# An expert layer on one core: a loop over experts, and an unrolled program with two chunks of the second product in plain fp32

## The reference, what is computed

```python
h = gelu(x @ Wi[e] + bi[e])          # 64x256 @ 256x1024
o = h @ Wo[e] + bo[e]                # 64x1024 @ 1024x256
r = o + x
y = (r - mean(r)) * rsqrt(var(r) + 1e-12) * gamma[e] + beta[e]
```

## Time and profile before

| What | Value |
|---|---|
| Median of three runs | 149.77 us |
| Span of the profiled execution, first to last instruction | 147.0 us |
| Busy PE / DVE / ACT / POOL | 118.9 / 115.8 / 76.2 / 68.8 us |
| DMA | 25.03 MB, mean 170 GB/s |
| Mean granted TensorE clock | 0.975 |

### The profile page before, as it was taken

The page is one execution under the profiler, slowest core; times in us unless marked ns, Lnnn a source line. Parts: engine busy times, 40 slices in busy tenths (PEclk is TensorE's granted clock), DMA queues, the critical chain, the costliest instruction groups (busy, mean ns, idle before and its releaser), DMA issues.

```text
span 147.0 us, 3876 instructions
## 1 busy us (share of the span) xinstructions
PE 118.9 (81%) x949; PEld 116.1 (79%) x949; DVE 115.8 (79%) x181; ACT 76.2 (52%) x126; POOL 68.8 (47%) x57
## 2 busy tenths in 40 slices
PE   0296968998999999497999979993999399977800
PEld 0195968997999999496999979992999299977800
DVE  2493457178988998995999699969996999679880
ACT  3022966677089408547933990299129912970000
POOL 3006570217614962404492659255925593570220
PEclk9999999999999999999999999999999968999995
DMA  4979996999818210293947488756124612020021
GB/s 108 384 214 357 342 322 139 287 384 302 327 37 276 57 36 18 72 379 98 311 84 303 113 282 264 245 119 233 34 71 121 211 33 66 13 60 18 0 55 36
DMA packets 17710, 25.03 MB, mean 170 GB/s; under 512 B 1616, under 2 KB 14480, under 8 KB 17552
## 3 DMA queue, kind: packets, MB, share of 16 engines
q10 hardware_dynamic: 9824, 14.42, 30.3%
q1 hardware_dynamic: 7856, 10.26, 23.1%
HBM read 22.58 MB, written 2.10 MB: 168 GB/s over the span
## 4 chain that ended last, share of the span: by engine, by line
issue 50%; POOL 20%; DMA 12%; POOLq 7%; SPq 6%; DVE 2%; DVEq 0%; PE 0%
POOL wo_lo L344 14%; DMA x_in<-x_dram 6%; POOL xs L355 6%; DMA bo_bc<-L_cond_bo_dram 5%; SPq L214 5%; POOLq L224 3%; POOLq L355 1%; DMA idx_i<-itok_B_dram 1%; SPq L224 1%; POOL rstd L362 1%; POOLq L56 1%; SPq L181 0%; POOLq L373 0%; POOLq L383 0%; POOLq L372 0%
## 5 line engine op out<-in xcount | busy, mean ns | idle before, releaser
L344 POOL TENSOR_TENSOR wo_lo<-wo_in,wo_hi 128x1024 fp32r<-128x1024 f32 x15 | 43.7, 2932 | 22.7 <-ACT wo_hi L425 22.7
L696 PE MATMUL preact<-xT_hi,wi_hi 128*128 128x256 f32 x144 | 42.1, 292 | 11.6 <-DVE wi_lo L569 6.1
L436 ACT ACTIVATE h<-preact,biT 128x256 f32<-128x256 f32 x72 | 28.3, 484 | 41.3 <-DVE h_lo L596 29.2
L596 DVE TENSOR_TENSOR h_lo<-h,h_hi 128x512 fp32r<-128x512 f32 x36 | 47.4, 1357 | 0.6 <-ACT h_hi L444 0.6
L696 PE MATMUL preact<-xT_lo,wi_hi 128*128 128x256 f32 x144 | 41.5, 288 | 0.0
L696 PE MATMUL preact<-xT_hi,wi_lo 128*128 128x256 f32 x144 | 41.4, 288 | 0.0
L696 PEld LDWEIGHTS preact<-xT_hi,wi_hi 128*128 128x128 f32 x144 | 28.3, 196 | 13.0 <-issue 13.0
L696 PEld LDWEIGHTS preact<-xT_hi,wi_lo 128*128 128x128 f32 x144 | 28.4, 197 | 0.0
L696 PEld LDWEIGHTS preact<-xT_lo,wi_hi 128*128 128x128 f32 x144 | 28.3, 197 | 0.0
L713 PE MATMUL sums_ps<-wo_hi,h_hi 128*128 128x256 f32 x144 | 23.9, 288 | 1.7 <-DVE r L537 1.6
L362 POOL TENSOR_TENSOR rstd<-var_eps,minus_half 128x2 f32<-128x2 f32 x9 | 8.6, 953 | 34.7 <-DVE var_eps L550 34.7
(11 more groups left out here) (57 smaller groups left out, 74.9 us busy)
## 6 DMA issues: line engine op xcount, KB each, us to landing
wo_in<-L_cond_Wo_dram ACTq DMA_DIRECT2D x7, 1024.0 KB, 6.1
wi_in<-L_cond_Wi_dram ACTq DMA_DIRECT2D x5, 1024.0 KB, 5.2
wi_in<-L_cond_Wi_dram SPq DMA_DIRECT2D x3, 1024.0 KB, 9.4
x_in<-x_dram SPq DMA_DIRECT2D x36, 64.0 KB, 2.8
y_dram<-xs SPq DMA_DIRECT2D x32, 64.0 KB, 2.1
bo_bc<-L_cond_bo_dram SPq DMA_DIRECT2D x1, 1024.0 KB, 7.0
wo_in<-L_cond_Wo_dram SPq DMA_DIRECT2D x1, 1024.0 KB, 6.6
gamma_bc<-L_cond_gamma_dram ACTq DMA_DIRECT2D x3, 256.0 KB, 5.6
```

What stands on the lines that cost most here:

```text
L344: nc.gpsimd.tensor_tensor(wo_half(wo_lo, e, half), wo_half(wo_in, e, half), wo_half(wo_hi, e, half).bitcast(FP32), ALU.subtract).then_inc( ...
L436: nc.scalar.activation(h[:, c, :], preact_chunk(c), ACT.Gelu, bias=biT[:, bass.ds(e * IC + c, 1)]).then_inc(gelu_done, 1)
L596: nc.vector.tensor_tensor(piece(h_lo, i), piece(h, i), piece(h_hi, i).bitcast(FP32), ALU.subtract).then_inc(h_lo_done, 1)
L696: last = nc.tensor.matmul(preact_chunk(c), w[:, e % 2, k, c * P:(c + 1) * P], xT[:, k, :], start=(k == 0 and w is wi_hi and xT is xT_hi), ...
```

## The change

The program is written anew, with the same arithmetic outside chunks 6 and 7 of the second product.

- **Straight code per block.** Up to 14 blocks are unrolled (`MIN_BLOCKS` 8 without a branch, then nested `If`). There is no loop over experts: every block has its own weights, loaded and split again for each block, with rings of 2 (Wi), 3 (Wo), 5 (vectors) and 6 (x).
- **Table.** It holds one sample number per slot (4 per block) and one expert per block. Empty slots point to spare rows behind the samples, and are loaded and stored too.
- **Inputs laid out by the host.** x is given also transposed, so the transposes on TensorE go; Wi, Wo and the vectors (bo, gamma, beta, bi) lie per expert as one row per partition.
- **Queues.** Everything after the first block's weights is issued by SP, each sample number read from the table just before its transfer.
- **Splits.** The gelu of chunks 0 to 5 writes back to PSUM; ACT copies the high part from there and DVE subtracts. Wo's low part moves from POOL to DVE, in two instructions of 1024 and 512 elements. POOL keeps the bias and the root, now per tile.
- **Chunks 6 and 7.** Their gelu goes to `h_raw` in SBUF, unsplit, and the second product takes them with the unsplit Wo in plain fp32: four matmuls per block in place of twelve.
- **TensorE's order.** Each block's first product is in four parts, with a quarter of the last block's second product behind each.
- **Warm-up.** 28 fp32 matmuls of 128 columns stand before the first block, where there were 12 and 6.

The diff, cut to its core:

```diff
--- before.py
+++ after.py
-            eng.dma_start(wi_in[:, e % 2, :, :], Wi[e, :, :].rearrange("(k p) n -> p k n", p=P)).then_inc(wi_loaded[e], 16)
...
+    WO_PIECES = [(0, IC // 2), (IC // 2, SPLIT_CHUNKS)]
+    WARM_UP = 28
+    WO_RING, PAR_RING, X_RING = 3, 5, 6
...
+        def entry(eng, at, hi, lo=0):
+            return eng.value_load(table[0:1, at:at + 1], min_val=lo, max_val=hi)
+        def sample(eng, t, j):
+            return entry(eng, QUAD * t + j, ROWS - 1)
...
+        def load_wo(eng, t, e):
+            if t >= WO_RING:
+                for piece in range(2):
+                    eng.wait_ge(wo_lo_done[piece], t - WO_RING + 1)
+                if RAW_BANKS:
+                    eng.wait_ge(sums_part, 4 * (t - WO_RING) + 4)
+            eng.dma_start(wo_in[:, t % WO_RING, :, :].rearrange("p c h -> p (c h)"),
+                          wo[bass.ds(e, 1), :, :].rearrange("o p f -> (o p) f")).then_inc(wo_loaded[t % WO_RING], 16)
+        def load_params(eng, t, e):
+            if t >= PAR_RING:
+                eng.wait_ge(y_ready, 2 * (t - PAR_RING) + 2)
+            eng.dma_start(params[:, t % PAR_RING, :],
+                          par[bass.ds(e, 1), :, :].rearrange("o p f -> (o p) f")).then_inc(par_loaded[t % PAR_RING], 16)
+        def load_xT(eng, t, slots=range(QUAD)):
+            if t >= 2:
+                eng.wait_ge(x_ready, t - 1)
+            for j in slots:
+                b = sample(eng, t, j)
+                eng.dma_start(xT_in[:, t % 2, j, :, :].rearrange("p k s -> p (k s)"),
+                              xt[bass.ds(b, 1), :, :].rearrange("o p f -> (o p) f")).then_inc(xT_loaded[t % 2], 16)
+        def load_x(eng, t):
+            if t >= X_RING:
+                eng.wait_ge(stored[t % X_RING], 4 * loads_of(t - X_RING, X_RING))
+            for j in range(QUAD):
+                b = sample(eng, t, j)
+                eng.dma_start(slot(t, j), xr[bass.ds(b, 1), :, :].rearrange("o s h -> (o s) h")).then_inc(
+                    x_loaded[t % X_RING], 16)
+        def store(eng, t, tile):
+            eng.wait_ge(y_ready, 2 * t + tile + 1)
+            for j in (2 * tile, 2 * tile + 1):
+                b = sample(eng, t, j)
+                eng.dma_start(out[bass.ds(b, 1), :, :].rearrange("o s h -> (o s) h"), slot(t, j)).then_inc(
+                    stored[t % X_RING], 16)
...
+        @block.sync
+        def _(sp):
+            sp.dma_start(idx_i[:, 0:B], idx.partition_broadcast(B)).then_inc(idx_loaded, 16)
+            sp.dma_start(idx_i[:, B:B + 1], idx.rearrange("(b o) -> b o", o=1)).then_inc(idx_loaded, 16)
+            sp.wait_ge(idx_loaded, 32)
+            load_params(sp, 0, sp.value_load(idx_i[0:1, 0:1], min_val=0, max_val=E - 1))
+            sp.wait_ge(table_ready, 1)
+            load_xT(sp, 0, (0, 1))
+            second = expert(sp, 1)
+            load_wi(sp, 1, second)
+            load_xT(sp, 1)
+            load_params(sp, 1, second)
+            load_x(sp, 0)
+            load_wo(sp, 1, second)
+            load_x(sp, 1)
+            n = entry(sp, T_BLOCKS, MAX_BLOCKS, MIN_BLOCKS)
+            def iteration(t, ahead):
+                if ahead:
+                    e = expert(sp, t + 2)
+                    load_xT(sp, t + 2)
+                    load_wi(sp, t + 2, e)
+                    load_params(sp, t + 2, e)
+                    load_x(sp, t + 2)
+                if t >= 2:
+                    store(sp, t - 2, 1)
+                if ahead:
+                    load_wo(sp, t + 2, e)
+                if t >= 1:
+                    store(sp, t - 1, 0)
+            def end(t):
+                iteration(t - 2, False)
+                iteration(t - 1, False)
+                store(sp, t - 2, 1)
+                store(sp, t - 1, 0)
+                store(sp, t - 1, 1)
+                for i in range(X_RING):
+                    sp.wait_ge(stored[i], 4 * 16 * len(range(i, t, X_RING)))
+            for t in range(MIN_BLOCKS - 2):
+                iteration(t, True)
+            from_block(sp, n, MIN_BLOCKS, lambda t, _: iteration(t - 2, True), end)
...
+            def residual(t):
+                pool.wait_ge(x_loaded[t % X_RING], 4 * loads_of(t, X_RING))
+                pool.wait_ge(par_loaded[t % PAR_RING], loads_of(t, PAR_RING))
+                for tile in range(2):
+                    nc.gpsimd.tensor_tensor(xs[:, t % X_RING, tile, :], xs[:, t % X_RING, tile, :], row(0, t),
+                                            ALU.add).then_inc(xs_ready, 1)
+            def root(t, tile):
+                pool.wait_ge(var_ready, 2 * t + tile + 1)
+                nc.gpsimd.tensor_tensor(rstd[:, tile:tile + 1], var_eps[:, tile:tile + 1], minus_half[:, :],
+                                        ALU.pow).then_inc(rstd_ready, 1)
+            def iteration(t, has):
+                if t >= 2:
+                    root(t - 2, 1)
+                if has:
+                    residual(t)
+                if t >= 1:
+                    root(t - 1, 0)
+            def end(t):
+                iteration(t, False)
+                root(t - 1, 1)
...
+            def gelu(t, q):
+                act.wait_ge(preact_ready, BANKS * t + q + 1)
+                if q == 0:
+                    act.wait_ge(par_loaded[t % PAR_RING], loads_of(t, PAR_RING))
+                if q == NS and t >= 2:
+                    act.wait_ge(sums_part, 4 * (t - 2) + 4)
+                for c in (2 * q, 2 * q + 1):
+                    pre = preact[:, q, (c % 2) * N:(c % 2 + 1) * N]
+                    to = pre if q < NS else h_raw[:, t % 2, c - SPLIT_CHUNKS, :]
+                    done = nc.scalar.activation(to, pre, ACT.Gelu, bias=params[:, t % PAR_RING, 3 * H + c:3 * H + c + 1])
+                done.then_inc(gelu_done, 1)
+            def h_high(t, q):
+                if q >= NS:
+                    return
+                act.wait_ge(gelu_done, BANKS * t + q + 1)
+                if t >= 2:
+                    act.wait_ge(sums_part, 4 * (t - 2) + 4)
+                nc.scalar.activation(h_hi[:, t % 2, 2 * q:2 * q + 2, :].rearrange("p c n -> p (c n)"), preact[:, q, :],
+                                     ACT.Copy).then_inc(h_hi_done, 1)
+            def iteration(t, has_next):
+                gelu(t, 0)
+                if has_next:
+                    wi_high(t + 1, 0)
+                h_high(t, 0)
+                gelu(t, 1)
+                if has_next:
+                    wi_high(t + 1, 1)
+                h_high(t, 1)
+                gelu(t, 2)
+                wo_high(t, 0)
+                h_high(t, 2)
+                gelu(t, 3)
+                wo_high(t, 1)
+                h_high(t, 3)
...
+            def h_low(t, q):
+                if q >= NS:
+                    return
+                dve.wait_ge(h_hi_done, NS * t + q + 1)
+                hi, lo = (x[:, t % 2, 2 * q:2 * q + 2, :].rearrange("p c n -> p (c n)") for x in (h_hi, h_lo))
+                nc.vector.tensor_tensor(lo, preact[:, q, :], hi.bitcast(FP32), ALU.subtract).then_inc(h_lo_done, 1)
...
+            def iteration(t, has_next, has=True):
+                if t >= 1:
+                    h_low(t - 1, 3)
+                    wo_low(t - 1, 1)
+                if t >= 2:
+                    centre(t - 2, 1)
+                if has:
+                    h_low(t, 0)
+                if t >= 2:
+                    finish(t - 2, 1)
+                if has_next:
+                    wi_low(t + 1, 0)
+                if has:
+                    h_low(t, 1)
+                if t >= 1:
+                    centre(t - 1, 0)
+                if has_next:
+                    wi_low(t + 1, 1)
+                if has:
+                    h_low(t, 2)
+                if t >= 1:
+                    finish(t - 1, 0)
+                if has_next:
+                    split_x(t + 1)
+                if has:
+                    wo_low(t, 0)
...
+            wi_low(0, 0)
+            wi_low(0, 1)
+            split_x(0)
+            wi_low(0, 2)
+            wi_low(0, 3)
+            for t in range(MIN_BLOCKS - 1):
+                iteration(t, True)
+            with_next(dve, n, MIN_BLOCKS - 1, iteration, end)
...
+            def second_product(t, part):
+                tile, half = part // 2, part % 2
+                if half == 0 and t >= 1:
+                    pe.wait_ge(sums_taken, 2 * (t - 1) + tile + 1)
+                tokens = slice(tile * P, (tile + 1) * P)
+                columns = sums_ps[:, tile, 0:H]
+                for c in range(half * IC // 2, (half + 1) * IC // 2):
+                    if c % 2 == 0 and tile == 0:
+                        if c < SPLIT_CHUNKS:
+                            pe.wait_ge(h_lo_done, NS * t + c // 2 + 1)
+                        else:
+                            pe.wait_ge(gelu_done, BANKS * t + c // 2 + 1)
+                    if c == half * IC // 2 and tile == 0:
+                        pe.wait_ge(wo_lo_done[half], t + 1)
+                    if c >= SPLIT_CHUNKS:
```

(93 more changed lines are left out.)

686 lines of the change are left out of this document (229 added, 457 removed).

## The result

The kernel after takes **172.19 us** (median of 4 runs, 171.34 to 173.9) beside 149.69 us for the kernel before on the same chip: ratio 1.152, 95% interval 1.143 to 1.162. The profiled execution has a span of 169.7 us, and its mean granted TensorE clock is 0.899 (0.975 before). I had forecast slower, 184 us, within 160 to 196.

A forecast was written before the change was run, and what follows sets the result against it. SP's queue was taken to bind, at 18.95 us per block over 12.85 of compute. Its issues up to the last Wi summed to 140.3 us; landing and tail gave a span of 181, so 184 us, range 160 to 196.

The forecast's parts named there:

- rival B: SP's queue still binds, but with a cheaper register load per sample transfer: 161 us, still slower; chance 0.06.
- A sample transfer, 1.34 us: SP's queue: one table read, its checks, address and transfer take 1.34 us; 12 per block, 84 up to the last Wi.
- A transfer without a read, 0.77 us: SP's queue: each transfer of Wi, Wo or vectors, needing no sample number, takes 0.77 us; 22 up to the last Wi.
- The sum to the last Wi: SP's queue up to the ninth block's Wi: table ready at 5.76, then 112.6, 5.0 and 16.9 us, together 140.3.
- SP's waits, nothing: SP's queue: loading two blocks ahead, it finds what it waits for done microseconds before, so its waits count as nothing.
- The tail, 41.2 us from that issue: After the last Wi's issue: landing 5.2 us later at 145.0, TensorE's last block from 155.3, norm and stores, end at 181.
- rival D: TensorE idles 7 us per block and stays at 1.2 GHz: 23.8 us a block, PE binds, 238 us; chance 0.04.
- Plain fp32 at 0.45 us a matmul: Second product's unsplit chunks on TensorE: 0.45 us per 256-column matmul, four taking 1.8 us where twelve fp32r took 1.4.
- DVE's blocking by POOL goes: Wo's low part leaves POOL, so about 4 us of mutual blocking per block go; low h takes 0.69 us.
- Rival A, 142.6 us if the queue doesn't bind: SP's queue doesn't bind; compute at 12.85 us per block sets the time, faster at 142.6 us; chance 0.14.
- the two rules weighed: Skill rules against trace rows on SP's queue: dispatch about 50 ns, not 0.502 us; register load about 600 ns, not 0.270.

The follow-up runs named there:

- e1: Four more unused register reads of the table on SP's queue in each pass that loads a block, against the kernel after: 186.11 us, ratio to before 1.234.
- e2: The kernel after, with SP reading each sample number once and keeping it in a register for the load of x and the store: 144.75 us, ratio 0.961.
- e3: The kernel after, with chunks 6 and 7 of the second product split like the others: 172.23 us, ratio 1.147.
- e4: The kernel after, with ACT issuing one more 512 KB load per block into a spare tile that nothing reads: 172.25 us, ratio 1.144.
- e8: As e6, with SP issuing the third block's Wi before the first two blocks' rows of x and the second Wo: 140.65 us, ratio 0.940.
- e5: As e2, with chunks 6 and 7 split as well: 148.31 us, ratio 0.989.
- e6: As e2, with DVE's split of the next x ahead of the first norm step in the pass: 142.66 us, ratio 0.952.
- e7: The kernel after, a read for each transfer kept, with the four stores of a block on ACT's queue: 151.91 us, ratio 1.013.

## Why the prediction was right, and where its sizes were off

The direction, the mechanism and the place are shown. SP's queue set the time: e1 lengthened it by register work alone, e2 shortened it by leaving register work out, e3 and e4 moved the rivals' causes and changed nothing. The size was forecast less well. The measured 172.19 us lies inside 160 to 196, but below the 174 to 195 that I gave the forecast by itself (no sum of mine led to the 174). What covers it is the room made for rival B, a cheaper read, and B's reason did not come: load, bounds and assertion are there and cost what they did. Something else was cheaper, the transfer of transposed x. The step by step comparison:

- **A sample transfer, 1.34 us.** Measured 1.25 for x and y, and 1.09 for transposed x (0.333 us of transfer, not 0.502, and 0.04 of address arithmetic, not 0.11). On the 34 transposed and 50 other transfers up to the last Wi that is 34 x 0.25 + 50 x 0.09 = 13 us too many. This term was mis-sized: I took one duration, that of 64 rows of 1 KB, for another form of transfer.
- **A transfer without a read, 0.77 us.** Measured about 0.51 to 0.56, 22 times, 5 us too many.
- **Left out:** 0.37 us before the first transfer of some passes and more where the first unrolled pass begins, and a slower issue now and then (up to 1.141 us). About 6 us too few in all, by what the other terms leave. The sum to the last Wi was 139.8 us, and the trace has 127.41.
- **SP's waits, nothing.** Right: none before 127.4. Its later waits for y, 7.6 us, lie in the tail.
- **The tail, 41.2 us from that issue.** Measured 169.7 - 127.4 = 42.3. Wi landed after 4.8 us where I took 5.2, TensorE began the last block 9.3 us after it (10.3 foreseen), and from there to the end it took 28.2 us (25.7 foreseen). Of these 2.5 us, 1.5 are its clock. It had stood idle for 3.3 us up to 141.49; the granted clock was 0.50 (1.2 GHz) from 143 to 145 us and 1.00 (2.4 GHz) again from 146. The stages (the number after the five busy times is the granted clock) and matmuls of the last block in the chain of waits:

```profile
141.00:145.00 4.00, 3.51 (x19) 3.51 (x20) 2.77 (x5) 1.06 (x3) 0.00 (x0) 0.65 0.10 26
145.00:148.00 3.00, 3.00 (x25) 3.00 (x25) 2.38 (x6) 0.78 (x3) 2.26 (x3) 0.90 0.18 44
...
143.01 0.21 PE preact L568
143.23 0.21 PE preact L583
143.44 0.21 PE preact L567
...
148.01 0.12 PE sums_ps L567
148.25 0.86 PE sums_ps L603 x4
```

  They stand 0.21 us apart up to 145.6 and 0.12 later. Sixteen of them at 0.09 more are 1.5 us. Another 0.5 is the wait for low Wo before the last block's own second product (0.82 us for 0.3). So rival D's mechanism was there, at a small size; TensorE came back within the block, as it had before.
- **Plain fp32 at 0.45 us a matmul.** The last row: four records, two matmuls, in 0.86 us, 0.43 each.
- **DVE's blocking by POOL goes.** Low h took 0.689 us in the mean of 27, with none of the 5.4 us pairs of the earlier trace rows. The gain was real and lay off the path of this kernel.
- **Rival A, 142.6 us if the queue doesn't bind.** e2 gave 144.75, with 12.41 us a block for 12.85 foreseen. The shorter block's gain was lost in the first passes, where ACT waits up to 4.4 us for the third block's Wi; e8 got part of that back.

So where did the expected gain of the new program go? It was there, about 6 us against the kernel before once the queue is relieved (e2, by the ratio), and 4 of them come from the unsplit chunks (e5). The queue's reads, 27 us, covered it and turned it into a loss.

Of the two rules weighed, the trace of after again had the sequencer held for 0.333 to 0.480 us per transfer on SP's queue, not the 50 ns that the Trainium skill ("DMA: Bandwidth & Descriptors", anatomy of one DMA) tells for the GpSimd path, and a register load took 0.268 us, not the 600 ns floor of its section on latency.

Open: what e6 would gain without the wait for Wo's low part, why the last block's Wi lands late in e8, and what the 2.72 us of ACT in e7 are; no run looked at them.

## What to carry to other kernels

Count what each queue issues per pass, reads of registers included, and multiply by rows of the trace, also for a queue that has no busy time in the table. A number read from SBUF cost its 0.57 us each time here; with the number kept in a register, transfers of x followed each other in 0.64 us in place of 1.25, as they share the address too. A saving on engines can only be judged once the bound has been looked for in the queues: e3 and e5 are the same edit, worth nothing in one kernel and 4 us in the other.

## What was not expected of the hardware

The time for which a transfer holds SP's queue differs from one to the next: in the kernel after 0.333 us for Wi, the vectors and transposed x (128 partitions of 512 B to 8 KB), 0.478 for x (64 rows of 1 KB), and 0.448 for Wo, though Wo has the size and form of Wi. Form alone doesn't fix it: in e2 the same Wo takes 0.344 and the same x 0.546. No run looked for the cause. ACT's queue issued a store during ACT's own instruction, so four reads and stores per block cost nothing there in the steady stage (12.42 us a block with them, 12.41 without).
